# A two-attention layer on one core: values in halves, one bank per reading, and a new planned order

## The reference

```python
# attention a: 16 heads of 8, with 32 more columns r that q and k share
q = concat([(x @ Wq + bq), r]); k = concat([(x @ Wk + bk), r])
attn = softmax(q @ k.T / sqrt(40)); x = x + (attn @ v) @ Wo + bo
# ffn: each token goes to the best of 8 experts, 128 -> 512 -> 128
y = sum(o * top1_mask) * top1_weight; x = x + y
# attention b: 16 heads, q1, q2, k1, k2 of 8 with rotary tables, values of 16
probs = softmax(q1 @ k1.T * s) - lam * softmax(q2 @ k2.T * s)
x = x + (probs @ v) @ W_proj
# the same ffn again
```

## Time and profile before

| what | us |
|---|---|
| median of 3 executions | 1688.32 |
| lowest, highest | 1685.33, 1711.72 |
| profiled execution | 1682.97 |
| its span | 1681.2 |

### The profile page before, as it was taken

One profiled execution on the slowest core, in us unless ns is written; L12 is line 12 of the kernel. 1 busy time (PEld: TensorE's weight loads), 2 busy tenths in 40 slices (PEclk: granted clock), 3 DMA queues, 4 the chain that ended last, 5 costly groups with the idle time before them and its releaser, 6 DMA issues.

```text
span 1681.2 us, 27841 instructions
## 1 busy us (share of the span) xinstructions
PE 1497.5 (89%) x9528; PEld 634.2 (38%) x9528; DVE 1179.4 (70%) x2107; ACT 1082.7 (64%) x1859; POOL 729.8 (43%) x794
## 2 busy tenths in 40 slices
PE   4699999999999989998999898899989988999836
PEld 2233333346643333554422231343334231544326
DVE  3587788777777787666677876667687786677524
ACT  2276766765657676766776775567777775676812
POOL 4302244235336453777464440343735500556313
PEclk9799999999999997999998896789999896999979
DMA  5854465857624247854111202632301114333022
GB/s 154 262 135 120 125 184 142 283 167 213 194 54 111 87 158 222 238 173 126 39 39 57 57 20 65 192 96 75 110 28 39 51 39 152 119 125 109 2 95 78
DMA packets 127795, 199.07 MB, mean 118 GB/s; under 512 B 16968, under 2 KB 95589, under 8 KB 127655
## 3 DMA queue, kind: packets, MB, share of 16 engines
q1 hardware_dynamic: 120694, 184.32, 36.6%
q0 software_dynamic: 6240, 12.71, 2.3%
q10 hardware_dynamic: 720, 0.26, 0.1%
HBM read 125.65 MB, written 73.46 MB: 118 GB/s over the span
## 4 chain that ended last, share of the span: by engine, by line
PE 72%; DVE 10%; ACT 7%; issue 3%; DMA 3%; SPq 2%; POOL 2%; ACTq 0%; POOLq 0%; DVEq 0%
PE ps L1118 21%; PE ps L1105 13%; PE ps L1084 12%; DVE Mb L1446 7%; ACT P L1294 6%; PE ps L1215 5%; PE ps L1202 5%; PE ps L1052 3%; PE ps L1126 3%; PE ps L1199 2%; PE ps L1213 2%; PE ps L1152 1%; PE ps L1171 1%; POOL ROW L1360 1%; PE ps L1068 1%
## 5 line engine op out<-in xcount | busy, mean ns | idle before, releaser
L1446 DVE TENSOR_REDUCE Mb<-ps 128x2 f32<-128x1024 f32 (+1 forms) x996 | 944.2, 974 | 377.4 <-PE ps L1084 373.3
L1294 ACT ACTIVATE P<-ps 128x512 f32<-128x512 f32 (+1 forms) x1113 | 809.3, 763 | 359.3 <-PE ps L1105 353.3
L1084 PE MATMUL ps<-STK 24*128 24x512 f16 (+1 forms) x1536 | 431.6, 404 | 52.4 <-DMA STK<-qka 17.8
L1105 PE MATMUL ps<-STK 25*128 25x512 f16 (+1 forms) x1536 | 426.1, 402 | 47.4 <-ACT P L1294 23.8
L1118 PE MATMUL ps<-P,V 128*32 128x512 f32 x3072 | 441.3, 649 | 5.0 <-ACT P L1294 4.7
L1105 PEld LDWEIGHTS ps<-STK 25*128 25x128 f16 (+1 forms) x1536 | 105.5, 94 | 299.9 <-ACT P L1294 101.0
L1084 PEld LDWEIGHTS ps<-STK 24*128 24x128 f16 (+1 forms) x1536 | 104.5, 95 | 299.9 <-DVE Mb L1446 92.0
L1720 POOL TENSOR_TENSOR TH<-TH,Z 128x512 f32<-128x512 f32 x65 | 82.5, 1270 | 108.5 <-ACT Z L1340 107.7
L1713 POOL DMA_INDIRECT xs<-ROW,slot x64 | 63.4, 990 | 108.9 <-DVE slot L1536 90.6
L1118 PEld LDWEIGHTS ps<-P,V 128*32 128x32 f32 x3072 | 62.0, 111 | 127.2 <-issue 112.7
L1202 PEld LDWEIGHTS ps<-XT,WE 128*128 128x128 f32 x752 | 103.2, 199 | 5.3 <-issue 1.0
(11 more groups left out here) (168 smaller groups left out, 1423.8 us busy)
## 6 DMA issues: line engine op xcount, KB each, us to landing
WE<-in_we SPq DMA_DIRECT2D x94, 576.0 KB, 4.0
STK<-qka SPq DMA_DIRECT2D x64, 480.0 KB, 5.9
qka<-HL SPq DMA_DIRECT2D x96, 256.0 KB
STK<-qkb SPq DMA_DIRECT2D x64, 256.0 KB, 2.7
qkb<-HL SPq DMA_DIRECT2D x96, 128.0 KB
X<-xs SPq DMA_DIRECT2D x84, 129.5 KB, 3.0
xs<-pad SPq DMA_DIRECT2D x8, 1036.0 KB, 6.4
qka<-HL SPq DMA_DIRECT2D x48, 128.0 KB
```

Of the source, the lines that this page charges most:

```text
L1084: mm = eng.matmul(ps[:, bank + i, :], l_, r_, start=True, stop=True)
L1105: mm = eng.matmul(ps[:, bank + i, :], l_, r_, start=True, stop=True)
L1294: eng.activation(P[:, st % 3, j:j + n, :], ps[:, bank:bank + n, :], ACT.Exp, scale=SCALE_A if g < 4 * B else SCALE_B).then_inc(sem("exp"), 1)
L1446: eng.tensor_reduce(Mb[:, g % 2, at:at + 4 * n - 3:4], ps[:, bank:bank + n, :], AX, ALU.max).then_inc(sem("mx"), 1)
```

## The change

Four things change.

1. The value step `pv` is split into `pv_half` and `pv`: the first does queries 0 to 255 of all four heads, the second 256 to 511. Only the second tells others that the step is done. Each is a step of its own in the order.
2. `fill_pair` always asks for one bank, so each `rowmax` and `expo` reads one bank.
3. The planner's costs and delays get other values, as do the costs of a single reading; the 0.3 us that steps outside the main five waited before they could be placed is gone.
4. The planner keeps a time for each quarter of the array's rows (`rows_free`): 24-row matmuls on different quarters may overlap, on the same quarter they follow each other, and a step that uses the whole array waits for all four.

The core of the diff (of the table of costs the lines for TensorE alone):

```diff
 STAGES = {
-    "smax": ("tensor", 0.216), "score": ("tensor", 0.216), "pv": ("tensor", 1.0), "mrow": ("tensor", 0.11), "oturn": ("tensor", 0.45),
+    "smax": ("tensor", 0.216), "score": ("tensor", 0.216), "pv": ("tensor", 0.52), "pv_half": ("tensor", 0.52), "mrow": ("tensor", 0.11), "oturn": ("tensor", 0.45),
...
-HOP = {"tensor": 0.13, "vector": 0.08, "scalar": 0.12, "gpsimd": 0.12, "sync": 0.05}
+HOP = {"tensor": 0.23, "vector": 0.13, "scalar": 0.14, "gpsimd": 0.15, "sync": 0.05}
...
+    rows_free = [0.0] * 4
...
     def fill_pair(rank, stage, *index):
 
-        yield ("do", rank, stage, index, 2 if index[-1] % 4 < 3 else 1, None, None)
+        yield ("do", rank, stage, index, 1, None, None)
...
+    def rows_of(stage, index, n):
+        if stage in ("smax", "score") and index[0] >= 4 * B:
+            return range(index[-1] % 4, index[-1] % 4 + n)
+        return range(4)
...
-                yield from do(g - 1.92 + c / 16, "rowmax", g, c, us=0.1 + 0.535 * n)
+                yield from do(g - 1.92 + c / 16, "rowmax", g, c, us=0.061 + 0.535 * n)
...
-                yield from do(st / 4 + j / 16, "expo", g, kt, j, us=0.14 + 0.37 * n)
+                yield from do(st / 4 + j / 16, "expo", g, kt, j, us=0.064 + 0.427 * n)
...
             yield from after(("exped", (g, kt)))
+            yield from do(st / 4 + 0.85, "pv_half", g, kt)
             yield from do(st / 4 + 0.85, "pv", g, kt)
...
-                t += 0 if stage in MAIN else 0.3
...
                 start = max(t, clock[e])
+                if e == "tensor":
+                    start = max([start] + [rows_free[r] for r in rows_of(stage, index, found[2] if bank else 1)])
...
-                us = n * (us if index[0] < 4 * B else 0.08)
+                us = n * (us if index[0] < 4 * B else 0.03)
...
+        more = 0.0
+        if e == "tensor":
+            taken = rows_of(stage, index, len(ring.get((stage, index), [0])))
+            more = 0.19 if len(taken) < 4 else 0.0
+            for r in taken:
+                rows_free[r] = start + us + more
...
-        end = start + us + LANDS.get(stage, HOP[e])
+        end = start + us + more + LANDS.get(stage, HOP[e])
...
-            def pv(g, kt):
+            def values(g, kt, half):
+
...
                 for j in range(4):
                     h = 4 * hh + j
-                    mm = eng.matmul(ps[32 * j:32 * j + 32, OB, :], V[:, b % 3, kt, vw * h:vw * h + 32], P[:, st % 3, j, :],
-                                    start=(kt == 0), stop=(kt == 3))
-                mm.then_inc(sem("pv"), 1)
+                    mm = eng.matmul(ps[32 * j:32 * j + 32, OB, 256 * half:256 * half + 256], V[:, b % 3, kt, vw * h:vw * h + 32],
+                                    P[:, st % 3, j, 256 * half:256 * half + 256], start=(kt == 0 and half == 0), stop=(kt == 3), skip_group_check=True)
+                return mm
+
+            def pv_half(g, kt):
+                values(g, kt, 0)
+
+            def pv(g, kt):
+                values(g, kt, 1).then_inc(sem("pv"), 1)
```

More of the change, by code:

```diff
@@ L161 @@
 STAGES = {
[L162 to L165 removed]
+    "smax": ("tensor", 0.216), "score": ("tensor", 0.216), "pv": ("tensor", 0.52), "pv_half": ("tensor", 0.52), "mrow": ("tensor", 0.11), "oturn": ("tensor", 0.45),
+    "hturn": ("tensor", 0.45), "feat": ("tensor", 0.86), "vproj": ("tensor", 1.0), "aturn": ("tensor", 0.45), "oproj": ("tensor", 1.3), "gturn": ("tensor", 0.45), "glogit": ("tensor", 0.8),
+    "gplace": ("tensor", 0.5), "xturn": ("tensor", 0.11), "up": ("tensor", 1.1), "down": ("tensor", 1.1),
+    "rowmax": ("vector", 1.13), "normal": ("vector", 0.6), "join": ("gpsimd", 0.8), "split": ("gpsimd", 1.6), "ln_stats": ("vector", 1.3),
     "ln_apply": ("gpsimd", 2.4), "ln_apply_q": ("vector", 1.45), "columns": ("vector", 3.0), "flo": ("vector", 0.63),
@@ L181 @@
 FROM = [(19.77, 0.27), (32.89, 0.43), (59.5, 0.9), (83.5, 0.55), (100.00, 0.10)]
-MAIN = ("smax", "rowmax", "score", "expo", "pv")
 ENGINES = ("tensor", "vector", "scalar", "gpsimd", "sync")
@@ L1219, in _ @@
             stages = dict(hturn=hturn, feat=feat, vproj=vproj, smax=smax, mrow=mrow, score=score,
-                          pv=pv, oturn=oturn, aturn=aturn, oproj=oproj, gturn=gturn, glogit=glogit, gplace=gplace, xturn=xturn, up=up,
+                          pv=pv, pv_half=pv_half, oturn=oturn, aturn=aturn, oproj=oproj, gturn=gturn, glogit=glogit, gplace=gplace, xturn=xturn, up=up,
                           down=down)
```

11 lines of the change are left out of this document (4 added, 7 removed).

## The result

The changed kernel takes **1887.01 us** (median of 4, 1883.0 to 1889.23), the kernel before beside it 1688.94 (1685.33 to 1711.72). The ratio is **1.118, 95% interval 1.115 to 1.121**: slower by 12%, outside the range of the prediction. The profiled execution took 1883.0 us, its span 1881.3.

A forecast was written before the change was run, and what follows sets the result against it. First stage is TensorE's own time, the second about a fifth waiting. First +24, second +60 + 35 - 143 = -48, together -24 us from 1682.97: 1659 us, range 1600 to 1725.

The forecast's parts named there:

- part 3: Single-bank readings on VectorE and ScalarE: splits cost 16 and 30 us, both hidden in idle time; banks come back earlier.
- part 4: New order in the second stage: waits for maxima, exponentials and issue fall from 215 to 72 us, -143 us.
- its 79 us: VectorE's price for splitting pairs of maxima by the skill's DRAIN section, set aside for 16 us from the trace.
- Part 1: Value steps in two halves: a half costs 0.665 us, each step 0.235 more; first stage +30, second +60 us.
- the +24: First stage in sum: 30 us for separate halves less 6 us of waits given back; ends +10 and +32.
- Part 2: Score matmuls apart in the second stage: 305 more runs, bounds 0 and +66 us, taken as +35 us.
- a return of 20 us in one rival: Rival that waits nearly vanish: full clock returns 20 us in the second stage, 1592 us in all; chance 0.22.
- the signs listed: Expected: second-stage maxima and exponentials below 10% of chain, VectorE's score idling well under 257 us, first stage 20 to 30 longer.
- TensorE becomes the bound: Rival, second stage: planner underprices halves, readers wait as before, 1718 to 1748 us; chance 0.18 for above 1706.

The follow-up runs named there:

- g1: Kernel before, own order and pairs kept, each pair of row maxima read by two instructions and released together: ratio 1.008.
- e3: Kernel before with single-bank readings alone (one planner line), old costs and whole value steps: ratio 1.088.
- e2: Kernel before with value steps in halves alone, old costs and pairs of banks kept: ratio 1.027.
- e1: Changed kernel, order kept word for word, with the whole value step in the place of the second half: ratio 1.056, 1806 us.
- e4: Kernel before with the new costs, delays and row quarters in the planner alone, whole value steps and pairs kept: ratio 0.967.
- e8: Changed kernel with pairs of banks back, new costs and halves kept: ratio 0.991.
- g2: Kernel before, own order kept, row maxima handed over bank by bank in both directions: ratio 1.002.
- h1: Kernel before with single-bank readings, plus a planner rule placing a value step only after all four scores of the next key tile: ratio 1.046.
- g3: Kernel before with new planner costs alone (the order of e4), maxima and exponentials both handed over bank by bank: ratio 0.982.
- h2: g3 plus the planner rule placing a value step only after all four scores of the next key tile: ratio 0.951, 1612.75 us.
- f3: Changed kernel with 18 added matmuls of a zero tile at each of 16 places in thin stretches of the second stage: ratio 1.135.
- e9: Changed kernel's order, both halves of a value step issued one behind the other in the place of the second: ratio 1.077.
- e5: e4 with a planner that also prices each change of tile shape at 0.095 us, value step put at 0.91: ratio 1.036.

## Why the prediction was wrong

**The step that failed is part 3 and its echo in part 4: that single readings are hidden on VectorE and ScalarE, and that the order of single banks only takes waits away.** In the sum these are 46 us hidden, nothing for the order, and -143. Their instruction prices were right: twelve maxima follow each other at 0.60 (7.28 less 0.68, by 11; 0.59 predicted), and g1 pays 14 us. (Timeline after.) The section that part 3 names for its 79 us, "The DRAIN you can't avoid" of "VectorE: DVE Perf Modes" in the Trainium skill, goes on to say that an operation that is not held starts earlier; the 0.60 against a duration of 0.68 agrees with that.

```profile
308.18 7.28 DVE L1466 TENSOR_REDUCE Mb<-ps 128x1 f32<-128x512 f32 x12
```

But I looked for the cost on the engines that read, and it is on the engine that writes. Asked for one bank at a time, the planner placed single score matmuls and value steps close behind them. Part 3 put that at nothing; the profiled e3 shows 61 us at full rate and, at 0.35 each, 111 us by 317 more at the lower level, and by the table's last column, against the kernel before beside it, 67 and 85 us (242 more). The planner saw no cost in that: it plays no clock.

**Part 1** had the right price for a half. The half near 305 us takes 0.57 to the next piece and has 0.31 ahead of it (timeline after, first stage):

```profile
304.81 0.38 PE L1118 MATMUL ps<-STK 121*128 121x512 f16 x1
305.12 0.64 PE L1132 MATMUL ps<-P,V 128*32 128x256 f32 x8
305.69 0.39 PE L1097 MATMUL ps<-STK 120*128 120x512 f16 x1
```

The first stage grew by 44 us, not 24. Halves alone (e2) make it 535 against 508, 27 us, which is the +24 (in the changed order they add only 9, 552 against e1's 543). The costs alone make it 520 (e4), singles alone 513 (e3), and both of these in the changed order 543 (e1): I had given the new order no price in this stage. In the changed kernel TensorE issues 274 us of score runs there, 25 more than before, as a run of alternating maxima and scores is now cut into ones and twos.

**Part 2**, +35 us for more and shorter runs, was of the right kind: the trace has 782 runs of score matmuls in the second stage and 1619 changes of tile shape, 475 and 1058 before. With part 1 it is in the 40 us at full rate; apart they were not measured.

**Part 4** predicted that the waits would fall from 215 to 72 us, -143. They halved: 7.5% of 1161 us for the two lines and 1.6% "issue" make 106. But the second stage at full rate is 40 us longer all the same, where part 4 with parts 1 and 2 had 48 less, and the clock fell from 0.91 to 0.79, which added 104. What left the chain as waits came back as TensorE's own time. The prediction knew the lower level only as a return of 20 us in one rival. The row was there: the earlier trace rows has a value step at 1.87 us against 0.99, and 0.91 over a stage of 1000 us is 180 us at the lower level. Its 20 us for all of that would be 63 at 0.35. I asked what the change would give back of it, and never what would make it grow. Of the signs listed, the chain's share came below 10% as forecast; VectorE's idle time for scores, which should have been well under 257 us, was 281; the first stage grew by more than 20 to 30; and the mean clock went the other way.

Of the rivals, "TensorE becomes the bound" had the right side and, in the first order, the right reason, but priced it at the full clock, 1718 to 1748. With the 104 us that the lower level adds, its upper end would be 1852, with 1887 measured.

**What stays open.** That the order made of single banks is the cause is shown (e3 and e8 against g1 and g2). That one rule on it takes half of the loss away is shown too (h1 against e3); that it does so by the lead is likely, but a new rule moves much else in the order, and the lead does not order all kernels: h1 has 4.2 and its clock falls 2.6 times per 100 us at the full level, the kernel before 1.9 times at a lead of 2.6, and g3 and h2 1.1 and 1.4 times at 2.6 and 4.9. The other half of the single banks' loss is not explained: h1 still stands at 1.046. Why halves cost twice as much beside single banks is open, and so is what makes the stretches at the lower level long.

The trace shows when the level changes: in the changed kernel TensorE had idled 0.6 to 1.8 us in the few us ahead of each of the second stage's 11 falls (it idles 4% of the time at the full level), most of all in groups without expert work, and ahead of 9 of the 11 rises it had not idled. The Trainium skill, "TensorE: Matmul & The Clock Gate", section "A second HAM failure mode: psum-queue depth-cycling", says that a kernel which cycles through PSUM banks can idle briefly and often enough between groups of matmuls for the clock to oscillate. By that section this kernel is a case of it, and the trace agrees as to the fall; it differs in that the clock of the changed kernel does not only oscillate but stays down, 137 us in one piece. Why it stays down is argued. Spaced at half speed, the two readers also get their banks late, so they hand them back late, and the stream does not become dense again: the long stretches are consistent with that loop, and f3's 101 us, won by 288 zero matmuls, with a way out of it. Against it stands that TensorE is busy 75.4 of the 79.9 us of groups 76 to 79 at the lower level.

## What to carry to other kernels

Write the time at the lower clock of each stage beside its waits before costing a change, since 2 x (1 - granted clock) x length reads it off one row; a planner or a sum that plays only durations and waits is blind to it, and here it was 104 of some 200 us. An engine that hides an operation does not hide the order which that operation brings: try the new order with the old instructions, and the new instructions in the old order (for the maxima here 0.2 to 0.8% against 7.3%). And where one engine fills buffers that two others empty, try a lead of one whole tile between producer and consumer in the plan itself: one rule was worth 3 to 4% in both orders it was tried in.

## What the hardware showed that I had not expected

- A us at the lower level costs 0.35 us here by the columns streamed (an estimate) and 0.32 to 0.39 between executions of the kernel before, not 0.5.
- The value steps of the same four groups (76 to 79) take 46.8 us with pairs of banks (e8) and 79.9 with single ones, one line of the planner apart.
- Two halves of a value step back to back cost 2.0% over a whole one (e9, e1), half or more of it by a lower clock.
- An order with fewer changes of tile shape (e5, 792 against e4's 1086 in the second stage) had a worse clock, 321 against 205 us at the lower level.
